# A scan's input products over 128 rows in place of 96

## What is computed

```
def step(h, inp):
    dt, b, xt, c = inp
    dA = jnp.exp(dt[:, :, None] * A)
    h = dA * h + dt[:, :, None] * b[:, None, :] * xt[:, :, None]
    y = jnp.einsum('bdn,bn->bd', h, c)
    return (h, y)
```

## Time and profile before

| | |
|---|---|
| median of 3 runs | 1306.98 us (1302.53 to 1307.23) |
| span of the profiled execution | 1301.5 us |
| PE busy, mean granted clock | 1102.2 us (85%), 0.93 |
| DVE busy | 820.0 us (63%) |
| ACT busy | 508.0 us (39%) |
| POOL busy | 308.2 us (24%) |

### The profile page before, as it was taken

The page is one execution under the profiler, slowest core; times in us unless marked ns, Lnnn a source line. Parts: engine busy times, 40 slices in busy tenths (PEclk is TensorE's granted clock), DMA queues, the critical chain, the costliest instruction groups (busy, mean ns, idle before and its releaser), DMA issues.

```text
span 1301.5 us, 29730 instructions
## 1 busy us (share of the span) xinstructions
PE 1102.2 (85%) x12064; PEld 704.2 (54%) x12064; DVE 820.0 (63%) x999; ACT 508.0 (39%) x1253; POOL 308.2 (24%) x930
## 2 busy tenths in 40 slices
PE   3637888889888888888884899999999598999998
PEld 2525444444544454444442677888887255475565
DVE  5858999999999999999995121111111566342111
ACT  3865555566555665566652111111111111212110
POOL 9741222222233222432244011111111200000000
PEclk9765899898899999998997899999999798999999
DMA  3798345443223222322214922232200400000000
GB/s 108 237 279 229 79 101 129 128 112 93 55 45 93 60 54 50 87 53 51 51 53 189 326 77 97 101 102 101 80 17 13 133 1 1 1 9 8 17 17 17
DMA packets 171833, 112.31 MB, mean 86 GB/s; under 512 B 93653, under 2 KB 162264, under 8 KB 169392
## 3 DMA queue, kind: packets, MB, share of 16 engines
q1 hardware_dynamic: 163264, 88.95, 24.4%
q0 software_dynamic: 8000, 20.87, 4.9%
q10 hardware_dynamic: 432, 0.59, 0.2%
HBM read 63.44 MB, written 45.90 MB: 84 GB/s over the span
## 4 chain that ended last, share of the span: by engine, by line
PE 49%; DVE 26%; issue 14%; SPq 5%; ACT 4%; DMA 2%; POOL 1%; DVEq 0%; ACTq 0%; POOLq 0%
DVE h L1159 20%; PE psum L1410 11%; PE psum L1422 11%; PE psum L1922 8%; PE psum L1933 4%; PE psum L943 2%; PE psum L1865 2%; ACT decay L1044 2%; PE psum L929 2%; PE psum L910 1%; SPq L199 1%; SPq L278 1%; PE psum L1857 1%; PE psum L1909 1%; SPq L282 1%
## 5 line engine op out<-in xcount | busy, mean ns | idle before, releaser
L1159 DVE TENSOR_TENSOR_SCAN h<-decay,psum 128x1024 f32<-128x1024 f32 x256 | 565.0, 2266 | 13.3 <-ACT psum L1054 7.8
L1044 ACT ACTIVATE decay<-psum 128x512 f32<-128x512 f32 x512 | 279.2, 600 | 195.9 <-PE psum L910 190.6
L929 PE MATMUL psum<-xdiag,bstat 96*128 96x64 bf16 x4096 | 175.6, 199 | 58.1 <-DVE h L1159 55.5
L929 PEld LDWEIGHTS psum<-xdiag,bstat 96*128 96x128 bf16 x4096 | 144.2, 102 | 84.5 <-DVE h L1159 77.2
L910 PEld LDWEIGHTS psum<-rows,shared 32*128 32x128 bf16 x4096 | 78.5, 96 | 181.7 <-issue 116.6
L943 PE MATMUL psum<-h,cstat 128*32 128x512 f32 x1024 | 149.0, 659 | 1.5 <-DVE h L1159 1.5
L1410 PE MATMUL psum<-xdt,shared 128*128 128x320 f32 x512 | 141.9, 439 | 0.7 <-ACT xdt L1469 0.7
L1422 PE MATMUL psum<-shared,hid 128*128 128x256 f32 x640 | 139.5, 379 | 0.6 <-ACT hid L1463 0.6
L1315 POOL TENSOR_TENSOR carry<-decay,h 128x16 f32<-128x16 f32 x240 | 58.2, 242 | 340.9 <-ACT decay L1044 340.6
L1422 PEld LDWEIGHTS psum<-shared,hid 128*128 128x128 f32 x640 | 121.0, 190 | 17.2 <-issue 1.1
L910 PE MATMUL psum<-rows,shared 32*128 32x64 bf16 x4096 | 109.9, 195 | 14.9 <-ACT decay L1044 7.6
(11 more groups left out here) (205 smaller groups left out, 1083.5 us busy)
## 6 DMA issues: line engine op xcount, KB each, us to landing
shared<-in_w SPq DMA_DIRECT2D x16, 1024.0 KB, 4.8
xdiag<-x_parts_d SPq DMA_DIRECT2D x256, 48.0 KB
x_parts_d<-x_parts POOLq DMA_DIRECT2D x46, 256.0 KB, 7.7
parts_d<-dt_parts SPq DMA_DIRECT2D x24, 256.0 KB, 8.6
rows<-parts_d SPq DMA_DIRECT2D x128, 48.0 KB
disp_d<-zero SPq DMA_DIRECT2D x4, 1305.0 KB, 8.2
xd<-disp_d SPq DMA_DIRECT2D x8, 652.5 KB, 6.2
picked_d<-zero SPq DMA_DIRECT2D x4, 1024.0 KB, 5.2
```

The costliest lines, as they stand in the source:

```text
L929: ins = pe.q.matmul(to.rearrange("p d (s e) -> p s d e", e=2), bstat[0:ROWS, c % 2, b, :], xdiag[0:ROWS, c % 2, b, :, d, :], start=True, s ...
L1044: act.q.activation(decay[:, gi % NB, 8 * half:8 * half + 8, :], per_d(bank_a[half]), ACT.Exp).then_inc(sem("exp"), 1)
L1159: dve.q.tensor_tensor_scan(out=h[:, half_slot(c, half), ch:ch + G, :].rearrange("p d t -> p (d t)"), data0=decay[:, gi % NB, :, :].rearran ...
```

## The change

The two operands of the input products are taken with all their partitions, where rows 0 to 95 were taken. Nothing else is edited; `first` (L969) keeps its 12 rows.

```
--- before.py
+++ after.py
@@ -926,8 +926,8 @@
                     d = slice(first_d(j, half), first_d(j, half) + 8)
                     for b in range(BLKS):
                         to = per_d(bank_in[gi % 2])[:, 8 * half:8 * half + 8, S * b:S * (b + 1)]
-                        ins = pe.q.matmul(to.rearrange("p d (s e) -> p s d e", e=2), bstat[0:ROWS, c % 2, b, :],
-                                          xdiag[0:ROWS, c % 2, b, :, d, :], start=True, stop=True)
+                        ins = pe.q.matmul(to.rearrange("p d (s e) -> p s d e", e=2), bstat[:, c % 2, b, :],
+                                          xdiag[:, c % 2, b, :, d, :], start=True, stop=True)
                 ins.then_inc(sem("inputs"), 1)
 
             def y(c, js):
```

## The result

| | before | after |
|---|---|---|
| median of 22 runs each | 1305.12 us | 1301.19 us |
| lowest to highest | 1300.01 to 1308.49 | 1297.69 to 1303.24 |
| span of the profiled execution | 1301.5 us | 1299.3 us |

The ratio is 0.9966, with a 95% interval of 0.9955 to 0.9977. What was forecast as nothing is a gain of 0.34%, 4.4 us by that ratio (the medians differ by 3.9): under the 0.5% that the prediction called different, but clear of noise with so many runs.

What follows compares the result with a forecast made beforehand. The scan stretch was taken as bound by DVE. The terms summed 0 + 0 + 0 + 0 = 0 us; the median 1306.98 less half a microsecond for fewer low stretches gave 1306.5 us, range 1300 to 1313.

Steps and rivals of the forecast that it cites:

- within 0.5%: Outcome class for the whole kernel's time, no change beyond what a measurement can tell (0.5%, 6.5 us): chance 0.87.
- the forecast with the spread of the runs: Whole kernel's time before the range was stretched: 1301.5 to 1311.5 us.
- rival 1: Scan stretch: the clock is held longer, -2 to -6 us, 1301 to 1305 us, likeliest 1304; chance 0.10.
- The bound: Scan stretch, 100.1 to 689.5 us: bound by DVE; PE changes can bring back at most its idle 8.1 us, 0.62%.
- (a): Time of the 4096 input products (L929): 0 ns; bounds -2 ns each, +10 at full clock or +18 at low.
- (b): The 4096 weight loads of the input products (L929): cost 0; bounds -3 and +0 ns each.
- rival 2: Input products (L929): time goes with rows, 7.8 us slower, 1314.8 us, +0.6%; chance 0.06.
- (c): Decay products (L910) beside the input products, no fourth strip left free: cost nothing; upper bound 1.2 us, lower 0.
- (d): Granted clock in the scan stretch: 0 taken, bounds 0 and -8.1 us; more low windows, costing 1 to 1.5 us, not excluded.

Runs made afterwards that it cites:

- rows128: The changed kernel once more (128 rows in the input products), against the kernel before: ratio 0.9971, median 1299.08 us against 1303.08.
- rows72: Kernel before with the input products cut from 96 to 72 rows, result not the reference's: ratio 1.0619, median of all runs 1396.3 us against 1303.1.
- awake96: Kernel before, input products still 96 rows, the two 128 x 512 products of stay_awake cut to 96 rows: ratio 1.0044, median 1312.43 us against 1306.44.
- zeroed72: Kernel before, 96 rows still named, but x not loaded for two of eight tokens, so moving-operand rows 72 to 95 stay zero: ratio 0.9971.

## Why the prediction was right, and where it was not

The time, the range and "within 0.5%" held; the sum did not. It was 0 us, and a gain of 4.4 us is there (0.34%). That the time held is in part luck: the step that decides it was put at nothing, and it was small. The measured 1301.19 us lies under 1301.5, the lower end of "the forecast with the spread of the runs", and is in the range because that had been stretched towards rival 1.

- The bound held. DVE sets the end of the stretch, what PE can give back is DVE's idle time, and the 8.1 us put as a cap was not passed: after kept 6.2 of it, rows128 4.3.
- (a) and (b) held at 0: 193 and 98 ns, 0.64 us a block, as stated under what would show it. So rival 2 did not happen. It was right in one point only, that low-clock groups have no room.
- (c) held at 0 within what can be seen: with 97 rows the fourth strip is taken and the time is 1.0002 (0.9985 to 1.0019), and the decay products last as long as before and stand as close to the input products. By the rule of the Trainium skill named there ("TensorE: Matmul & The Clock Gate", Part 3, on what overlaps), a taken row group should have cost something. No run here shows it: the loads of 128 rows still start about 28 ns apart in a block while products on the same rows are in flight.
- (d) is the step that failed. I wrote that no row separates work on many rows from work on few, took 0 and gave the case 0.10 as rival 1. The runs separated it: at the same columns and instructions the clock follows the rows named, and not the values (0.929 with 96 rows, 0.943 with 128, 0.813 with 72, and 0.930 with 96 of which 24 are zeros). Rival 1's price was right, -2 to -6 us with 1304 as the likeliest; the medians differ by 3.9 us. The mechanism was named and weighed too low. The reason given against it, "nothing shows rows counting", was the absence of a test and not evidence. The same paragraph's other half, that more rows might make the clock fall more often, is refuted: 0.943 against 0.929.
- Of the signs, the counts were poorer than the idle time: I put the low windows at 7 or fewer for rival 1, and the two profiles of 128 rows have 8 and 5. ACT's waits for L929 (26 times, 10.7 us before) are 24 and 10.5, which says nothing: a copy that waits delays a scan only if DVE is already idle, so the scan's own wait (7.8 to 4.4 us) was the row to name.
- The base was a little high: the median of 22 runs of before is 1305.12, not the 1306.98 of the first three. Of the 5.3 us between 1306.5 and 1301.19, 1.4 are the base and 3.9 the gain.

On the clock the same page of the Trainium skill, in Part 1, lets the gate follow how busy PE has recently been. The direction agrees with these runs: more of stay_awake, more clock. But by busy time alone rows72 would have kept the clock of before, as PE's work is the same in columns and instructions. The measured clock is 0.813 against 0.929, and there the measurement decides.

That the clock is the way by which the rows act is shown by its going with them through seven heights while a product of L929 lasts the same at a given level of the clock, whatever its height (189 to 193 ns at the shortest in all, 242 at the longest, 238 with 64 rows), and by awake96, which reaches the same end from another product (0.910 against 0.927). Not shown is how the chip weighs rows against columns, and whether weight loads or products or both are what it sees: they name the same rows in every kernel here.

## What to carry over

Before trimming the height of a matmul, or leaving it trimmed, look whether the granted clock has low stretches in which its products lie on a path without room; zero rows cost nothing in the products' time here (193 ns with 96 rows and with 128) and hold the clock up. The size is not symmetric: where the clock was already full in 41 of 52 windows, 32 rows more brought 0.3%, and 24 fewer cost 6%. Extra products to hold the clock are a different thing: they take PE's time in order, and once per group was already too much where PE and ACT hand work to each other in a ring.

## What I had not expected of the hardware

- Products of 72 rows in place of 96, with the same columns, took the mean granted clock from 0.929 to 0.813 and the median time up by 7% (64 rows: 0.755 and 13%), without one product being longer at a given clock.
- No effect of the values was seen: 24 rows with zeros in the moving operand counted like 24 rows of data (zeroed72, clock 0.930), and ones in place of zeros in 32 rows changed nothing (0.942 against 0.941 and 0.943).
- It goes more finely than by strips of 32: 97 rows as 96 (0.930, 0.929), 112 between 96 and 128 (0.938), and 84 and 72 rows, which touch three strips like 96, well below it (0.866, 0.813).
